# Ternary weights of the feed-forward layer: from VectorE to GpSimd, in eight pieces at other places

## The reference

```
def weight_quant(w):
    scale = 1.0 / jnp.clip(jnp.mean(jnp.abs(w)), 1e-05)
    return jnp.clip(jnp.round(w * scale), -1, 1) / scale
def bit_linear(x, w):            # act_quant: round(x * 127 / max|x|) per token
    return jnp.einsum('bsd,hd->bsh', act_quant(x), weight_quant(w))
...
x = x + tanh(g_xattn) * xattn(layernorm(x), ctx, ctx, Wq, Wk, Wv, Wo)
h = bit_linear(layernorm(x), w1)          # 256 -> 1024
h = silu(depthwise_conv1d(h))             # 3 taps along the sequence
x = x + tanh(g_ffn) * bit_linear(h, w2)   # 1024 -> 256
```

## Time and profile before

| what | value |
|---|---|
| device time, three runs | 237.27, 234.13, 236.86 us; median 236.86 |
| span of the profiled execution, first to last instruction | 235.2 us; no other time of it is given |
| span against the median of the runs | 1.7 us below |
| TensorE, VectorE, ScalarE, GpSimd busy | 92%, 81%, 69%, 52% of the span |
| mean granted TensorE clock | 0.984 |

### The profile page before, as it was taken

One profiled execution on the slowest core, in us unless ns is written; L12 is line 12 of the kernel. 1 busy time (PEld: TensorE's weight loads), 2 busy tenths in 40 slices (PEclk: granted clock), 3 DMA queues, 4 the chain that ended last, 5 costly groups with the idle time before them and its releaser, 6 DMA issues.

```text
span 235.2 us, 6424 instructions
## 1 busy us (share of the span) xinstructions
PE 215.8 (92%) x2439; PEld 180.1 (77%) x2452; DVE 190.4 (81%) x387; ACT 161.9 (69%) x318; POOL 122.2 (52%) x229
## 2 busy tenths in 40 slices
PE   7999999997999999999999999989985699997974
PEld 7887787886878787887878878768783588886963
DVE  4163548789798999999999999999899859999671
ACT  2557768777687888989889788667933356674741
POOL 2421326364365757668677576657567224433470
PEclk9999999999999999999999999999999589999999
DMA  5982011010110101100000000000000000111111
GB/s 168 370 270 67 3 49 38 10 46 3 45 47 3 46 3 45 40 11 22 3 3 3 3 0 3 1 3 0 3 0 0 24 25 22 47 46 45 49 52 60
DMA packets 9488, 9.86 MB, mean 42 GB/s; under 512 B 1010, under 2 KB 9202, under 8 KB 9458
## 3 DMA queue, kind: packets, MB, share of 16 engines
q1 hardware_dynamic: 9458, 9.46, 12.2%
HBM read 7.36 MB, written 2.10 MB: 40 GB/s over the span
## 4 chain that ended last, share of the span: by engine, by line
PE 68%; DVE 21%; issue 5%; ACT 3%; DMA 1%; POOL 1%; SPq 0%; ACTq 0%; DVEq 0%; POOLq 0%
PE ps_score L464 10%; PE ps_proj L430 8%; PE ps_proj L509 6%; PE ps_av L487 6%; PE ps_max L474 6%; PE ps_proj L422 5%; DVE zmax L1151 5%; PE ps_proj L413 4%; PE ps_h L568 4%; PE ps_av L707 4%; DVE y L1041 4%; DVE y L1044 3%; DVE smax L987 3%; PE ps_av L497 2%; PE ps_proj L401 2%
## 5 line engine op out<-in xcount | busy, mean ns | idle before, releaser
L987 DVE TENSOR_REDUCE smax<-ps_max 128x8 f32<-128x1024 f32 x31 | 37.9, 1223 | 13.9 <-PE ps_max L474 10.7
L789 ACT ACTIVATE prob<-ps_score 128x1024 f32<-128x1024 f32 x32 | 32.7, 1023 | 17.8 <-PE ps_score L464 16.9
L464 PE MATMUL ps_score<-Qs,KT 32*128 32x128 f32 x512 | 37.1, 283 | 2.0 <-DVE smax L987 0.8
L464 PEld LDWEIGHTS ps_score<-Qs,KT 32*128 32x128 f32 x512 | 31.3, 186 | 9.3 <-issue 5.0
L474 PE MATMUL ps_max<-KT,QT 32*128 32x256 f32 x248 | 35.1, 400 | 0.0
L359 POOL TENSOR_SCALAR zq<-y,zmax 128x1024 f16<-128x1024 f32 x16 | 17.9, 1119 | 29.1 <-issue 18.1
L1151 DVE TENSOR_REDUCE zmax<-y 128x1 f32<-128x1024 f32 x16 | 19.4, 1214 | 5.3 <-ACT y L935 5.3
L336 POOL TENSOR_SCALAR xn<-xn,qa 128x256 f32<-128x256 f32 x16 | 8.1, 508 | 28.1 <-DVE qa L1027 28.1
L829 ACT ACTIVATE y<-hid,conv 128x512 f32<-128x512 f32 x24 | 18.6, 807 | 4.3 <-DVE hid L1034 3.9
L707 PE MATMUL ps_av<-w2q,zqT 128*128 128x256 f16 x128 | 17.4, 281 | 4.3 <-ACT zqT L941 2.6
L474 PEld LDWEIGHTS ps_max<-KT,QT 32*128 32x128 f32 x248 | 21.1, 184 | 0.1
(11 more groups left out here) (140 smaller groups left out, 551.9 us busy)
## 6 DMA issues: line engine op xcount, KB each, us to landing
cin<-ctxT SPq DMA_DIRECT2D x16, 128.0 KB, 2.1
xres<-x SPq DMA_DIRECT2D x16, 128.0 KB, 2.5
out<-xres SPq DMA_DIRECT2D x16, 128.0 KB, 1.7
w1f<-w1T SPq DMA_DIRECT2D x1, 1024.0 KB, 6.2
w2f<-w2T SPq DMA_DIRECT2D x1, 1024.0 KB, 8.1
wk<-wkT SPq DMA_DIRECT2D x1, 256.0 KB, 2.8
wv<-wvT SPq DMA_DIRECT2D x1, 256.0 KB, 4.4
wq<-wqT SPq DMA_DIRECT2D x1, 256.0 KB, 4.6
```

The lines of the kernel that those rows point to most:

```text
L464: mm = pe.matmul(ps_score[:, i * 512 + j * P:i * 512 + (j + 1) * P], KT[b % 3][rows, j * P:(j + 1) * P], Qs[rows, j * P:(j + 1) * P], star ...
L789: act.activation(prob[pair][:, :], ps_score[:, :], ACT.Exp, scale=DH ** -0.5).then_inc(exp_done, 1)
L987: dve.tensor_reduce(dst, first_max(n, pair)[:, :].rearrange("p (g t e k) -> p g t e k", g=PG, t=KD, e=2), AX.X, ALU.max).then_inc(max_done, 1)
```

## The change

`ternary` is taken out of VectorE's program and put into GpSimd's, with the same three instructions per piece and the same waits. In steps 3 to 6 GpSimd does one piece after `norm2(s-2)`, ahead of `dequantise` and `round1(s-2)`, and one at the end of the step, after `x_mean(s+3)`: w1's pieces in steps 3 and 4, w2's in 5 and 6. VectorE keeps `weight_scale(0)` and `weight_scale(1)` at the end of steps 2 and 4. Nobody else's order changes.

```diff
@@ gpsimd
+            def ternary(k, wf, wt, i, step_done, done):
+                n = KD * HID // PIECES
+                wf, wt = wf[:, k * n:(k + 1) * n], wt[:, k * n:(k + 1) * n]
+                gp.wait_ge(scale_done, i + 1)
+                gp.tensor_scalar(wf, wf, w_scale[:, i:i + 1], 1.0, ALU.mult, ALU.min).then_inc(step_done, 1)
+                gp.wait_ge(step_done, 2 * k + 1)
+                gp.tensor_scalar(wf, wf, -1.0, ROUND, ALU.max, ALU.add).then_inc(step_done, 1)
+                gp.wait_ge(step_done, 2 * k + 2)
+                gp.tensor_scalar(wt, wf, ROUND, None, ALU.subtract).then_inc(done, 1)
+
+            first = (w1f, w1q, 0, wq1_step, w1q_done)
+            second = (w2f, w2q, 1, wq2_step, w2q_done)
+            pieces = {3: (0, first), 4: (2, first), 5: (0, second), 6: (2, second)}
             for s in range(NB):
                 if seq(s - 2):
                     norm2(s - 2)
+                if s in pieces:
+                    k, weight = pieces[s]
+                    ternary(k, *weight)
                 for T in TILES.get(s, ()):
                     if on_gp(T):
                         dequantise(T)
...
                     x_mean(s + 3)
+                if s in pieces:
+                    ternary(k + 1, *weight)
@@ vector
-            def ternary(k, wf, wt, i, step_done, done):
...
             step(2, lambda k: weight_scale(0) if k == 1 else None)
-            step(3, pieces(0, w1f, w1q, 0, wq1_step, w1q_done))
-            step(4, pieces(2, w1f, w1q, 0, wq1_step, w1q_done, scale=1))
-            step(5, pieces(0, w2f, w2q, 1, wq2_step, w2q_done))
+            step(3)
+            step(4, lambda k: weight_scale(1) if k == 1 else None)
+            step(5)
             dve.wait_ge(small_in, 16)
-            step(6, pieces(2, w2f, w2q, 1, wq2_step, w2q_done))
+            step(6)
```

## The result

| what | before | changed |
|---|---|---|
| device time, median | 236.57 us (234.13 to 237.27) | 268.11 us (267.97 to 268.65) |
| ratio to before, 95% interval | | 1.135 [1.131, 1.140] |
| span of the profiled execution | 235.2 us | 266.9 us |
| mean granted TensorE clock | 0.984 | 0.935 |

The change costs 31.5 us. The forecast was 245.7, in a range up to 250.0. The direction and the places were right; the size is off by a factor of 3.6.

What follows compares the result with a forecast made beforehand. TensorE, busy 92% of the span, was taken as the bound, with GpSimd's chain setting the deadlines. 2.7 + 3.1 + 0.8 + 2.2 = +8.8 us on 235.2 gives 244.0, plus 1.7 to the median: 245.7 us, range 241.0 to 250.0.

Steps and rivals of the forecast that it cites:

- The price of a piece on GpSimd: One ternary piece on GpSimd, called p: instructions of 0.69 + 0.64 + 0.62 plus three gaps of 0.1, 2.25 us.
- the bounds 1.6 to 4.1: Limits for a piece's price: 256-column prices below, three times the two-input 128x512 L350 above, each plus gaps.
- the signs of being wrong that the prediction names: Instructions under 0.45 us, a short ScalarE wait, or TensorE getting through steps 3 to 6 faster than before.
- Terms one and two: Late w1q in step 5 delays project_q(6), +2.7 us; late w2q and xn in step 7 delay w2_column_sums, +3.1.
- 3p - 4.05 and 3p - 3.65: Losses at the step 5 and step 7 deadlines as functions of p, the price of a piece.
- step 3's first piece as hidden: GpSimd's first piece in step 3 fits into its wait for qrec_done and costs nothing.
- The wait before `project_out(3)`: TensorE's 1.06 us wait in step 4, put down to VectorE's w_mean, goes once the piece ahead leaves VectorE.
- Term three: Step 7: norm1(8) and the last piece slowed beside VectorE's outer taps by the shared port, +0.8 us (0 to 1.3).
- Term four: TensorE's clock falls to half after the new stands in steps 5 and 7: one fall counted, 2.2 us.
- the prediction's own case: Pieces of 2.25 us, both stalls, clock falls at least once: 245.7 us, chance 0.60.
- A piece is dear: Rival: each 0.1 us of piece price costs 0.6; 2.6 gives 247.8 us, 4.1 gives 256.8; chance 0.08.
- No gain behind step 7, none from VectorE's relief: After step 7 TensorE bounds as before, nothing given back or added; no way to a gain over 2%.

Runs made afterwards that it cites:

- Experiments 3 and 5: 3: changed kernel, pieces written as multiply and add, cuts left out: 244.88 us; 5: changed kernel, same result, rounding first, then min-max cut: 244.19 us.
- the variants with cheap pieces: Changed kernel with pieces rewritten to some 2.2 us: multiply-add without cuts 244.88 us; rounding first 244.19; that with later w1r copies 241.08, and later w2_column_sums 236.75.
- experiment 6: Changed kernel with dummy identity matmuls keeping TensorE busy in its four stands of steps 5 and 7: 264.30 us.
- experiment 8, the last kernel: Changed kernel with rounding first, ScalarE's w1r copies moved to steps 7 and 8, and w2_column_sums one step later: 236.75 us, ratio 1.002.
- the variant with cheap pieces and late copies: Changed kernel with rounding first (pieces of 2.2 us) and ScalarE's two w1r copies moved to steps 7 and 8: 241.08 us, ratio 1.019.

## Why the prediction was wrong

- **The step that failed** is "The price of a piece on GpSimd": "I take 2.25, since the two rows of the same instruction bracket it on both sides." The rows were of another pair of operations. L336, L343 and L359 are all mult-add or add-mult; the change's are mult-min, max-add and a lone subtract. The interpolation over columns was good (0.69 and 0.62 measured for those forms), and the error was all in the operations: the three instructions took 2.02, 1.93 and 1.49 us where 0.69, 0.64 and 0.62 were assumed. The true p is 5.7, outside the bounds 1.6 to 4.1: the upper one came from an instruction of another class, and no row excluded more. It should have been called open above. None of the signs of being wrong that the prediction names is a dear instruction. Experiments 3 and 5 show that this step is the cause: with pieces of 2.2 us at the same places the kernel takes 244.9 and 244.2.
- **Terms one and two** were mis-sized by p: 2.7 and 3.1 forecast, 13.1 and 13.4 us of stands measured. The places and the waits were right, and 3p - 4.05 and 3p - 3.65 give 13.0 and 13.4 at 5.7. That they agree to 0.1 us is partly luck. The first takes step 3's first piece as hidden, which fails above a price of about 3.65 and accounts for the 1.24 us in step 4; against it, norm2(2) took 1.9 instead of 2.0, round1 to x_mean 3.1 instead of 3.2, and 0.66 us of slow TensorE work fill a part of the wait. The second holds nothing for the shared port, of which 1.3 us lie in its chain.
- **The wait before `project_out(3)`** did not go, against the prediction: with p = 5.7 `xn2` came so late that `quantise1(2)` delayed `w_mean`, 1.99 us. In the variants with cheap pieces it went. VectorE's row:

```profile
58.33 0.42 DVE L1039 TENSOR_REDUCE qa<-xn 128x1 f32<-128x256 f32 x1 [2.38 <-POOL xn L330]
```

- **Term three**, the shared port: 0.8 forecast. In the change two instructions of norm1(8) beside VectorE's outer taps took 0.65 and 1.08 instead of 0.19 and 0.57, part of the 8.44, and L370 of the last piece 2.24 instead of 1.94, part of the 5.00: 1.3 us together. That it is the port that is shared is argued from which instructions overlap; no run took the taps away.
- **Term four**, the clock: one fall at 2.2 us forecast, two that count seen, 3.8 us together (experiment 6), so 1.9 each on the mean. In the prediction's own case, experiment 3, there were two falls as well.
- **The rivals.** "A piece is dear" was the one that happened, beyond its far end; its slope, 0.6 us for each 0.1 of p, gives 245.7 + 20.7 = 266.4 for 5.7, and 268.3 with the second fall; that is reckoned afterwards and leaves out the seventh piece, so part of its closeness to 268.1 is luck. The rival had 0.08.
- **No gain behind step 7, none from VectorE's relief** was right (experiment 8, the last kernel).

## What to carry to other kernels

Before work goes to another engine, look for rows there of the very same operations; on GpSimd a factor of three lies between mult-add and mult-min at equal size, and a bound from other operations is none. Then walk the receiving engine's chain to each deadline as a function of the unknown price: the walk mostly outlives a wrong price, and the slope (here six pieces of eight) says how much the range must widen. Write down as well at which price each hidden piece stops being hidden, since the slope changes there (here a seventh piece from 3.65 us on). If the longest wait in a trace is released by an engine that has hardly any idle time itself, expect next to nothing from moving the waiting instruction (here 0.6 us for a wait of 14.2).

## What was not expected of the hardware

- GpSimd's tensor_scalar with float32 in, 512 columns: 0.61 to 0.70 us for mult-add, add-mult, mult-mult and min-max; 1.49 to 1.57 for a single mult, add, subtract, min or max; 1.93 to 2.04 for mult-min, max-add, add-min, add-add, mult-subtract and subtract-mult. Two operations can be cheaper than one: adding a constant alone took 1.49, adding it and multiplying by 1 took 0.62.
- The other engines' work hardly changed these prices: 2.02, 1.94 and 1.49 in steps 3 to 6, 2.03, 1.94 and 1.50 behind the end. The exceptions lay beside VectorE's outer taps in step 6's last piece: max-add 2.24 instead of 1.94 in the change, add-mult 1.10 instead of 0.62 in experiment 3.
- The stands of 6.3 and 5.0 us in the change were followed by 3.5 us each at a granted clock of 0.50; dummy products in the stands kept it at 1.00 and gave back 3.8 us (experiment 6). Not every stand is followed by a fall: in the variant with cheap pieces and late copies one of 2.85 us was followed by 1.00.
